# A graph layer on one core: the one-hots of the low source parts with the 128 nodes innermost

## The reference

```python
h      = relu(layernorm(x))                                  # per node
deg    = max(count of edges by dst, 1)
weight = (deg[src] * deg[dst]) ** -0.5                       # per edge
msg    = (h[src] + relu(edge_attr @ W1e + b1e) @ W2e + b2e) * weight
agg    = segment_sum(msg, dst)                               # back to nodes
y      = relu(((1 + eps) * h + agg) @ W1n + b1n) @ W2n + b2n + h
out    = x + y * rsqrt(mean(y * y) + 1e-7) * rms_w
```

## Time and profile before

| | us |
|---|---|
| median of three runs | 1082.5 |
| profiled execution, own time | 1078.76 |
| its span (first to last instruction) | 1076.9 |
| PE busy | 962.5 (89%) |
| PE weight loads busy | 795.8 (74%) |
| DVE busy | 910.1 (85%) |
| POOL busy | 756.9 (70%) |
| ACT busy | 652.7 (61%) |

### The profile page before, as it was taken

One profiled execution on the slowest core, in us unless ns is written; L12 is line 12 of the kernel. 1 busy time (PEld: TensorE's weight loads), 2 busy tenths in 40 slices (PEclk: granted clock), 3 DMA queues, 4 the chain that ended last, 5 costly groups with the idle time before them and its releaser, 6 DMA issues. The chain is left out here.

```text
span 1076.9 us, 35614 instructions
## 1 busy us (share of the span) xinstructions
PE 962.5 (89%) x12752; PEld 795.8 (74%) x12752; DVE 910.1 (85%) x4063; ACT 652.7 (61%) x1747; POOL 756.9 (70%) x754
## 2 busy tenths in 40 slices
PE   0324999999999999999999999999999999999985
PEld 0323788888888887887887888788788788888753
DVE  6998888888888878888887888887888898888668
ACT  7962666666666666656665666665666566666435
POOL 2045777777777777777777777777777777777475
PEclk9999999999999999999999999999999999999988
DMA  6045544544544544454454454454445445442483
GB/s 239 15 176 178 167 127 138 162 130 137 163 131 138 155 139 142 140 152 144 122 170 137 128 167 130 139 152 140 141 141 154 142 126 168 142 123 75 159 298 104
DMA packets 57741, 156.99 MB, mean 146 GB/s; under 512 B 16052, under 2 KB 23399, under 8 KB 57185
## 3 DMA queue, kind: packets, MB, share of 16 engines
q1 hardware_dynamic: 33776, 104.43, 27.9%
q0 software_dynamic: 22784, 47.07, 18.4%
q10 hardware_dynamic: 1008, 3.21, 0.9%
HBM read 147.95 MB, written 6.70 MB: 144 GB/s over the span
## 5 line engine op out<-in xcount | busy, mean ns | idle before, releaser
L1063 POOL DMA_INDIRECT arena<-node_rows,idx x712 | 712.4, 1001 | 228.9 <-issue 139.9
L1234 ACT ACTIVATE arena<-bank 128x294 f16<-128x294 f32 x900 | 328.5, 422 | 266.3 <-PE bank L1139 260.0
L1224 ACT ACTIVATE arena<-bank 128x512 f32<-128x512 f32 x405 | 222.6, 596 | 104.8 <-PE bank L1089 98.5
L1149 PE MATMUL bank<-t_words,arena 128*120 128x256 f16 x2205 | 282.6, 275 | 0.4 <-DVE arena L1352 0.4
L1289 DVE TENSOR_SCALAR arena<-iota_c,code 128x294 f16<-128x294 f16 x900 | 273.7, 359 | 2.3 <-PE bank L1139 2.3
L1302 DVE SCALAR_TENSOR_TENSOR arena<-iota_h,hi_f,bank 128x49 f32<-128x49 f32 x900 | 184.1, 261 | 61.9 <-PE bank L1104 59.9
L1149 PEld LDWEIGHTS bank<-t_words,arena 128*120 128x120 f16 x2205 | 233.8, 133 | 0.6 <-issue 0.6
L1139 PE MATMUL bank<-arena 128*128 128x294 f16 x900 | 206.1, 307 | 23.2 <-DVE arena L1289 17.7
L1089 PEld LDWEIGHTS bank<-w1e,arena 64*128 64x128 f32 x3240 | 215.6, 190 | 4.7
L1089 PE MATMUL bank<-w1e,arena 64*128 64x128 f32 x3240 | 218.1, 272 | 0.0
L1139 PEld LDWEIGHTS bank<-arena 128*128 128x128 f16 x900 | 101.4, 144 | 84.7 <-DVE arena L1289 35.4
(11 more groups left out here) (208 smaller groups left out, 802.5 us busy)
## 6 DMA issues: line engine op xcount, KB each, us to landing
arena<-in_attr SPq DMA_DIRECT2D x90, 512.0 KB
arena<-low_src SPq DMA_DIRECT2D x47, 652.5 KB, 7.5
arena<-node_rows,idx POOLq DMA_INDIRECT x712
arena<-in_attr SPq DMA_DIRECT2D x45, 128.0 KB
node_rows<-arena SPq DMA_DIRECT2D x1, 3160.5 KB, 8.9
arena<-in_x ACTq DMA_DIRECT2D x7, 448.0 KB, 11.0
arena<-in_x SPq DMA_DIRECT2D x6, 512.0 KB, 12.4
out<-arena SPq DMA_DIRECT2D x12, 224.0 KB
```

The source lines that it names most:

```text
L1063: nc.gpsimd.indirect_dma_start(out=edge_rows[:, u, j, 0:ROW], out_offset=None, in_=table, in_offset=bass.IndirectOffsetOnAxis(ap=idx[:, c, ...
L1149: mm = nc.tensor.matmul(x_sum[0:XC, 0:2 * D], strip[:, u, k, :], T16[:, k, :], start=k == 0, stop=k == NBLK - 1)
L1224: nc.scalar.activation(out.rearrange("p (j o) d -> p o j d", o=2), z[:, :, j0:j0 + n // 2, :], ACT.Relu).then_inc(r_ready, 1)
L1234: nc.scalar.activation(strip[:, u, :, tile * W:tile * W + W], pair_bank[:, j * 512:j * 512 + CW].rearrange("p (k w) -> p k w", w=W), ACT.C ...
```

## The change

The sets of `low_oh` lie as (tile, node), with the 128 nodes innermost, so that a tile's weights are 128 values side by side. `iota_l` is one row of 128 numbers rather than 128x10, and L1286 reads it again for each tile. The low part of a tile, which was read from ten values side by side, is now one value read 128 times before the next. The number of instructions and their order stay as they were on every engine.

```diff
-        iota_l = sb("iota_l", [128, 128, LB], F16)
+        iota_l = sb("iota_l", [128, 128], F16)
-        loop.low_oh = take(2 * LB * 128 // 2).bitcast(F16).rearrange("p (u n t) -> p u n t", u=2, t=LB)
+        loop.low_oh = take(2 * LB * 128 // 2).bitcast(F16).rearrange("p (u t n) -> p u t n", u=2, t=LB)
-            numbers(iota_l[:, :, :], [[1, 128], [0, LB]])
+            numbers(iota_l[:, :], [[1, 128]])
@@ count_pair
-                    nc.tensor.matmul(pair_bank[:, j * 512:j * 512 + CW], low_oh[:, low_set(c, p), :, 2 * p % LB + j], code_oh[:, (c * NA + p) % PB, j, :, 0:W],
+                    nc.tensor.matmul(pair_bank[:, j * 512:j * 512 + CW], low_oh[:, low_set(c, p), 2 * p % LB + j, :], code_oh[:, (c * NA + p) % PB, j, :, 0:W],
@@ pair
-                    nc.vector.tensor_tensor(low_oh[:, low_set(c, p), :, :], here.unsqueeze(1).broadcast_to((128, 128, LB)),
-                                            iota_l[:, :, :], ALU.is_equal)
+                    nc.vector.tensor_tensor(low_oh[:, low_set(c, p), :, :], here.unsqueeze(2).broadcast_to((128, LB, 128)),
+                                            iota_l[:, :].unsqueeze(1).broadcast_to((128, LB, 128)), ALU.is_equal)
```

## The result

The changed kernel takes 1128.5 us (median of four runs, 1126.31 to 1131.38), the kernel before 1082.62 in the same comparison (four runs): a ratio of 1.0404, with a 95% interval of 1.0375 to 1.0433. The forecast was 1125 with a range of 1098 to 1146, slower. Set against each other they differ by 52.6 us, the medians by 45.9.

The account below looks back on a forecast made before the run. PE was taken to bound 21 steps and POOL's chain of gathers 24. Terms of 3.6, 7.8, 27.6 and 3.6 made 42.6 us over the profiled 1078.76, so 1121.4; 3.7 for the median gave 1125 us, range 1098 to 1146.

Parts of the forecast that it names:

- L1286 at 1.49 us: DVE's low one-hot write: reading one value repeatedly unpacks it, 0.67 us more, twice a step, from 0.82 us.
- The PE-set step at 20.7: Steps set by PE: 0.67 us more before pair 5, 0.22 less for weight loads, so 20.24 grows by 0.45.
- The POOL-set step at 21.8: Steps set by POOL: gathers held by longer L1286, 0.64 in phase 4 and 0.51 in phase 1, 1.15 over 20.62.
- POOL sets the step from about the eighth: Early loop: POOL loses 1.75 us per step rather than 1.05, so it takes over from PE about step eight.
- The sum in the loop: Over the loop's 45 steps: 3.6 early, 7.8 for five turned POOL-set, 27.6 middle, 3.6 end; 42.6 us more.
- Around the loop: Outside the loop: no cost counted; the prologue's shorter row on POOL (4.17 us) gives nothing, as POOL next waits 20.20 us.
- POOL not held up: Rival: gathers on POOL aren't held by the longer L1286, only PE's chain grows; 1097 us, chance 0.11.
- Staying packed: Rival: L1286 on DVE keeps its packed rate, only weight loads change, 4.6 us faster; 1078 us, chance 0.05.
- Hidden by DVE's spare time: Rival: the 1.34 us fits in DVE's 2.7 idle per step, no change; 1082 us, chance 0.04.
- The slower read: Rival: L1286's repeated read on DVE takes 2.37 us, steps some 23.5; about 1225 us, chance 0.04.
- The bad phases: Rival: gathers caught at L1286's start, 29 steps cost 0.8 us more each; 1148, upper part of the 0.74 main case.
- The page's rule on ports: DVE and POOL: two-port modes block GpSimd, so neither form of L1286 would; prediction said the trace disagrees. No size given.

Follow-up runs that it names:

- e2: Kernel before with its old layout, but the number row read with each value repeated ten times, so L1286 is unpacked; 1361.35 us, ratio 1.0232 to the kernel before.
- e1: Changed kernel's layout with each low part stored twice and read as pairs, against the kernel before; 1332.75 us against 1331.21, ratio 1.0012.
- l1: Kernel before with most of PE's edge MLP and strip products left out, against the whole kernel before; 1067.45 us against 1083.27, ratio 0.9858.
- l2: Changed kernel with most of PE's edge MLP and strip products left out; 1119.6 us, ratio 1.0363 to the whole kernel before, 52.2 us more than l1.
- y0_before: The kernel before run once more with nothing changed, used as its second profile; 1081.86 us.
- e4: Changed kernel with L1286 of pairs 5 to 9 moved ahead of phase 1's look-up wait; 1327.69 us, ratio 0.9975 to the kernel before.
- l3: Low one-hots by ten one-source instructions, PE's work thinned as in l1 and l2; 1083.22 us, ratio 0.9999 to the whole kernel before.
- the first two sets: Two comparison sets of changed-kernel runs and variants with whole PE work, each against the kernel before of its own set, which took 1331 us.
- the third set: Comparison set with l1, l2 and l3, PE's work thinned, run where the kernel before takes 1083 us.

## Why the prediction was right, step by step

- **L1286 at 1.49 us.** 1485 ns, 90 times. The rate came from L604, the only row that shares the repeated value. (Its own numbers give (1091 - 150) / 896 = 1.05 rather than 1.04 ns per value, which leaves the 1.49.) e2 shows that it is the repetition in the innermost dimension of either operand, e1 that the same values read in pairs cost nothing. The Trainium skill (Vector Engine (DVE) Microarchitecture Reference, Performance modes — why throughput varies by op and dtype) had the rule, one result per cycle where a repeated row keeps two. This trace agrees with the ratio: (1485 - 150) / 1280 = 1.04 ns per value, against 0.52 before.
- **The PE-set step at 20.7.** 20.73 and 20.70. Its parts in the trace: 0.71 more wait at pair 5 (0.89 - 0.18), and 0.25 less for the count products, which makes the 0.46 by which the step grows. Start to start, six of the twenty products got shorter, by 0.04 each: the first of each of the five pairs behind fp32 products, and one more. The prediction had five at 0.045, 0.22. Its reason, that fp32 passes keep the load back, is too wide: behind L1089 the load of L1139 starts only with the product itself, but behind L1162 and L1175, fp32 too, it starts 0.11 us ahead of it.
- **The POOL-set step at 21.8.** 21.73 over 28 steps, and the holding shown alone by l1 and l2. Of the 91 gathers that begin beside an L1286 and more than 0.12 us from its end, 90 take 0.94 us and what L1286 has left by then, to 0.03. Summed over the middle steps, L1286 of phase 4 holds them for 0.69 us per step (0.02 before) and that of phase 1 for 0.64 (0.11 before). These are +0.67 and +0.53, where the prediction had 0.64 and 0.51. The other two-source instructions hold 0.11 less than before, which it had not counted, and so the held time grew by 1.09 and the step by 1.11, near its 1.15.
- **POOL sets the step from about the eighth.** It does from the tenth, and DVE waits for gathers as forecast.
- **The sum in the loop.** From the first L1286 of phase 1 to the last it is 894.26 us before (104.11 to 998.37) and 936.23 after (106.68 to 1042.91), 42.0 more. The forecast had 42.6, and its parts hold too: eight early steps +3.8 (3.6 forecast), the 29 in which POOL comes to set the step +34.1 (7.8 + 27.6 = 35.4), the end +3.5 (3.6). That it is so close is partly luck of the profile. In the second one of the kernel before, y0_before, the same stretch takes 890.29 us (105.53 to 995.82), and its steps stay near 20.3 to the nineteenth and not the twelfth, so the count of 24 POOL-set steps is of one execution. Against it the loop grew by 45.9.
- **Around the loop.** The profiled executions differ by 52.6 us, 10.7 of them outside this stretch: 2.6 ahead of it and 8.1 behind it. The prediction priced both at nothing. The timeline of the kernel before, from the last L1286 of phase 1 to the start of the node MLP behind a barrier:

```profile
998.37 0.82 DVE L1286 TENSOR_TENSOR arena<-lo_h,iota_l 128x1280 f16<-128x1280 f16 x1
...
1027.33 5.96 POOL L827 TENSOR_TENSOR arena<-acc,arena 128x512 f32<-128x512 f32 x4 [17.15 <-POOLq L880]
```

the same of the changed kernel:

```profile
1042.91 1.48 DVE L1286 TENSOR_TENSOR arena<-lo_h,iota_l 128x1280 f16<-128x1280 f16 x1
...
1056.96 0.95 POOL L1063 DMA_INDIRECT arena<-node_rows,idx  x1 [0.30 <-issue]
1059.88 0.39 DVE L1330 TENSOR_TENSOR arena<-arena 128x128 f32<-128x128 f16 x1 [3.04 <-DMA arena<-node_rows,idx]
1064.56 0.38 DVE L1330 TENSOR_TENSOR arena<-arena 128x128 f32<-128x128 f16 x1 [4.29 <-DMA arena<-node_rows,idx]
...
1079.98 5.95 POOL L827 TENSOR_TENSOR arena<-acc,arena 128x512 f32<-128x512 f32 x4 [22.08 <-POOLq L880]
```

and of the kernel before once more, y0_before:

```profile
995.82 0.82 DVE L1286 TENSOR_TENSOR arena<-lo_h,iota_l 128x1280 f16<-128x1280 f16 x1
...
1007.95 0.94 POOL L1063 DMA_INDIRECT arena<-node_rows,idx  x1 [0.30 <-issue]
...
1014.91 0.39 DVE L1330 TENSOR_TENSOR arena<-arena 128x128 f32<-128x128 f16 x1 [3.99 <-DMA arena<-node_rows,idx]
...
1030.25 5.96 POOL L827 TENSOR_TENSOR arena<-acc,arena 128x512 f32<-128x512 f32 x4 [21.35 <-POOLq L880]
```

The two pass 28.96 us apart before and 37.07 after, where DVE waits 3.04 and 4.29 us for the last rows. It looks as if POOL's late gathers cost 8.1 us here. But in y0_before, with nothing changed, DVE waits 3.99 us for the last rows too, and the stretch takes 34.43. So 5.5 of the 8.1 us are found between two executions of the same kernel, and at most the other 2.6 can be laid to the change. The last gather starts 14.05 us behind L1286 after, 12.13 in y0_before and 10.87 before, so POOL's lateness may well be their cause; that isn't shown. Against y0_before the changed kernel is 49.5 us longer, 45.9 of them in the loop; by medians the whole difference is 45.9.

- **The rivals.** POOL not held up (1097) fell by the 1.65 and 1.85 us gathers and by l2. Staying packed fell by the 1485 ns. Hidden by DVE's spare time fell by the steps of 20.70 and 21.73 us: L1286 of phase 4 is hidden on PE's way, as the prediction had it, and that of phase 1 is not, unless it is moved as in e4. The slower read fell by 1485 ns against 2.37 us. The bad phases came true in single steps only.
- **The page's rule on ports.** The prediction set two-port modes against the trace, and was right that they don't explain it, but it had missed the page that fits. The Trainium skill (SBUF — State Buffer, SBUF: two separate sides) says that a VectorE instruction competes for the pair of ports shared with GpSimd also when it has two SBUF inputs, then only against a GpSimd instruction that reads SBUF, and that whichever starts first has the pair for its whole length. A gather reads its row numbers (`idx`) from SBUF. By that rule L1286 blocks in either form. The trace agrees: gathers are held to the end of L1286 (1.65, 1.85, 2.12 us) and of L1294 (1.10), and beside L1316 (1.40, where the end of the three instructions would give 1.44). L1302, one of whose tensors is in PSUM (`bank`), holds none: 43 gathers that met it in the changed kernel took 0.94 to 0.95. In one point the trace differs: a gather that starts just ahead of L1286, as that at 489.64 does by 0.09, is not held, but it doesn't hold L1286 either, which takes its 0.82 all the same. One-source writes held no gather for more than 0.06 us (0.94 beside L1274, 0.96 beside ten writes in l3). Whether the engine runs them in a two-port mode no run shows, so they test the two-port rule only as far as the prediction went.

## What to carry to other kernels

Ask of a layout change what the operand's innermost dimension does to the instruction that writes it, before what it gives to the one that reads it: here ten loads, each 43 ns shorter and mostly hidden, were bought with a write 667 ns longer and, once in a step, not hidden. In this kernel, where POOL issues gathers back to back, a vector instruction with two SBUF inputs can cost twice: on its own engine's way, and as time until its end for every gather it catches. So POOL's true spare time is what its fixed gaps leave and not its busy share. And profile the kernel before twice, before a difference outside the changed part is laid to the change: here 5.5 of 8.1 us behind the loop were there without it.

## What the runs showed of the hardware that was not expected

A wait of PE can be followed by a stretch at the lower clock. Timeline and window of the changed kernel (the window's last three figures: granted clock, DMA share, GB/s):

```profile
488.83 0.58 PE L1139 MATMUL bank<-arena 128*128 128x294 f16 x2 [1.89 <-DVE arena L1289]
489.57 3.19 PE L1149 MATMUL bank<-t_words,arena 128*120 128x256 f16 x15
...
494.62 1.83 PE L1149 MATMUL bank<-t_words,arena 128*120 128x256 f16 x15
```

```profile
488.00:498.00 10.00, 9.17 (x110) 8.22 (x114) 8.91 (x39) 4.55 (x12) 7.87 (x8) 0.83 0.37 100
```

PE stood still for 1.89 us, and the fifteen strip products behind it took 3.19 us, where the next fifteen took 1.83. The granted clock is 0.83 over these ten microseconds, so part of them ran at the lower of its two levels, 1.2 GHz; it is 1.00 in the early steps. The changed kernel has seven such stretches in its loop, each behind a wait of 1.9 to 2.0 us at pair 5, and the kernel before, whose longest wait there is 1.1 us, has none in either profile. But eight other waits of 1.8 to 2.0 us were followed by none, so the wait alone doesn't decide it. Seven of the nine steps of 22.3 to 22.9 us have a fall in them and two do not, so how much of their length is owed to it was not separated; in the middle POOL sets the pace, and a slower PE matters only where it passes POOL.

The other thing is the 1331 us for the same kernel, with stops of about a microsecond in PE's stream. All 38 executions of the kernel before in the first two sets took 1328.5 to 1334.4 us, on chips 12 and 8, and all 13 of the third set 1078.0 to 1088.0, on chip 5. Whether it is the chip was not tested, and the cause stays open. It was of use all the same: in it one of two bounds was lifted, and what was left of the loss, 2.1% of 4.0%, belonged to the other.
